# Layer 1 of a two-layer transformer block: the minus-maxima of the second half move ahead of the keys and the gate product on TensorE

## What is computed

```python
x = x + L0_xattn(_layernorm(x), ctx, ctx, ...)
x = x + L0_ffn(_layernorm(x), ...)
x = x + L1_xattn(_layernorm(x), ctx, mask, ...)
x = x + L1_ffn(_layernorm(x), ...)

def L1_xattn(x, context, mask, ...):
    q, kv = ln(x) @ Wq, ln(context) @ Wkv
    k, v = split(kv)                       # with a null key and value ahead
    sim = einsum('bhid,bhjd->bhij', q * 0.25, k)
    attn = softmax(where(mask, sim, -big))
    return ln((attn @ v) @ Wo)

def L1_ffn(x, w_gate, w_up, w_down):
    gate = silu(bitlinear(x, w_gate))
    return bitlinear(gate * bitlinear(x, w_up), w_down)
```

## Time and profile before

| | us |
|---|---|
| median of 3 runs | 889.36 |
| lowest and highest of the 3 | 884.31, 891.05 |
| the profiled execution: its time | 892.16 |
| the profiled execution: its span, first to last instruction | 890.4 |
| PE busy in the span | 831.4 (93%) |
| DVE busy | 679.9 (76%) |
| ACT busy | 433.5 (49%) |
| POOL busy | 480.8 (54%) |

### The profile page before, as it was taken

The page is one execution under the profiler, slowest core; times in us unless marked ns, Lnnn a source line. Parts: engine busy times, 40 slices in busy tenths (PEclk is TensorE's granted clock), DMA queues, the critical chain, the costliest instruction groups (busy, mean ns, idle before and its releaser), DMA issues.

```text
span 890.4 us, 28136 instructions
## 1 busy us (share of the span) xinstructions
PE 831.4 (93%) x10019; PEld 683.1 (77%) x10019; DVE 679.9 (76%) x1920; ACT 433.5 (49%) x1011; POOL 480.8 (54%) x972
## 2 busy tenths in 40 slices
PE   4999999998599997999999999999999999999964
PEld 2777777777598885788888888888888888888842
DVE  3788888876534564678888888888888888888865
ACT  1566666545055663334445454554545545445432
POOL 7567678877422224336465564655646556464331
PEclk9999999988799997999999999999999999999985
DMA  8566330001556651112112121121211212112120
GB/s 252 213 253 260 134 103 14 15 20 41 161 152 164 162 156 30 35 33 58 37 49 53 35 65 38 47 55 36 64 38 50 53 35 65 37 46 49 29 59 9
DMA packets 57980, 71.33 MB, mean 80 GB/s; under 512 B 8051, under 2 KB 34547, under 8 KB 57843
## 3 DMA queue, kind: packets, MB, share of 16 engines
q1 hardware_dynamic: 42546, 45.08, 19.4%
q10 hardware_dynamic: 13248, 20.26, 6.2%
q0 software_dynamic: 2048, 4.20, 1.6%
HBM read 45.13 MB, written 24.38 MB: 78 GB/s over the span
## 4 chain that ended last, share of the span: by engine, by line
PE 87%; DVE 5%; issue 3%; DMA 2%; ACT 1%; POOL 1%; SPq 0%; ACTq 0%; DVEq 0%; POOLq 0%
PE psum L1708 7%; PE psum L1634 7%; PE psum L1733 7%; PE psum L1684 7%; PE psum L1625 7%; PE psum L1664 6%; PE psum L975 4%; PE psum L380 4%; PE psum L965 4%; PE psum L1744 4%; PE psum L1720 4%; PE psum L387 3%; PE psum L399 3%; PE psum L371 2%; PE psum L1698 2%
## 5 line engine op out<-in xcount | busy, mean ns | idle before, releaser
L1894 ACT ACTIVATE a_pT<-psum 128x512 f32<-128x512 f32 x128 | 69.5, 594 | 67.3 <-PE psum L1720 39.7
L667 DVE TENSOR_REDUCE l_mx<-psum 128x4 bf16<-128x512 f32 x128 | 81.5, 678 | 1.9 <-PE psum L371 1.8
L2037 DVE TENSOR_REDUCE a_mxf<-psum 128x4 f32<-128x512 f32 x128 | 81.2, 675 | 2.1 <-PE psum L1698 2.0
L1634 PEld LDWEIGHTS psum<-a_cTm,a_Wk 128*128 128x128 f32 x512 | 65.0, 197 | 22.8 <-issue 21.3
L1466 POOL TENSOR_TENSOR f_hd<-f_hmc,f_wmean 128x1 f32<-128x1 f32 x32 | 6.8, 212 | 137.1 <-DVE f_hr L2150 137.1
L1625 PEld LDWEIGHTS psum<-a_xT,a_Wq 128*128 128x128 f32 x512 | 66.1, 196 | 15.3 <-issue 14.4
L502 ACT ACTIVATE l_pT<-psum 128x512 f32<-128x512 f32 x128 | 70.5, 598 | 12.4 <-PE psum L387 12.1
L1708 PE MATMUL psum<-a_qT,a_kT 64*128 64x128 f32 x1024 | 73.5, 284 | 0.0
L1634 PE MATMUL psum<-a_cTm,a_Wk 128*128 128x128 f32 x512 | 70.7, 282 | 1.9 <-POOL a_cTm L1423 1.1
L1625 PE MATMUL psum<-a_xT,a_Wq 128*128 128x128 f32 x512 | 71.1, 283 | 0.5 <-ACT a_xT L1877 0.5
L1684 PE MATMUL psum<-a_Wv,a_cTm 128*128 128x512 f32 x128 | 70.1, 630 | 1.5 <-DVE a_kT L2025 0.7
(11 more groups left out here) (300 smaller groups left out, 2228.0 us busy)
## 6 DMA issues: line engine op xcount, KB each, us to landing
sorted_x<-r_zeros ACTq DMA_DIRECT2D x12, 1408.0 KB, 5.8
a_r_all<-a_r_rows SPq DMA_DIRECT2D x64, 256.0 KB, 4.0
e_w<-in_E_W1b SPq DMA_DIRECT2D x39, 258.0 KB, 2.8
e_xt<-sorted_x SPq DMA_DIRECT2D x39, 64.0 KB, 2.4
sorted_y<-e_yt ACTq DMA_DIRECT2D x39, 64.0 KB, 2.6
a_cin<-in_ctx SPq DMA_DIRECT2D x32, 64.0 KB
out<-f_x SPq DMA_DIRECT2D x32, 64.0 KB, 3.3
x_res<-in_x SPq DMA_DIRECT2D x1, 512.0 KB, 7.3
```

The source lines that it names most:

```text
L667: nc.vector.tensor_reduce(mx[:, s, Q4 * k:Q4 * k + Q4], maxp[k % 2].rearrange("p (h t) -> p h t", h=Q4), AX_X, ALU.max).then_inc(mx_ready, 1)
L1634: last = nc.tensor.matmul(bank[:, i * S:(i + 1) * S], Wk[:, 4 * half + i, :], cTm[:, b % 2, :], start=True, stop=True)
L1894: nc.scalar.activation(pT[:, 2 * half + e, :], tp[e], ACT.Exp, scale=SCALE).then_inc(exp_ready, 1)
L2037: nc.vector.tensor_reduce(mxf[:, hh:hh + 4], maxp[e].rearrange("p (h t) -> p h t", h=Q4), AX_X, ALU.max).then_inc(mxf_ready, 1)
```

## The change

On TensorE, `minus_max(b, 1)` is called right behind `values(b, 0)`, ahead of `keys(b + 1, 0)` and `gate_part(f)`. Nothing is added or removed, and the lists of the other engines and the waits inside the functions are as they were.

```diff
                 queries(b + 1, 0)
             if b >= 1:
                 values(b, 0)
+            minus_max(b, 1)
             if more:
                 keys(b + 1, 0)
             if f is not None:
                 gate_part(f)
-            minus_max(b, 1)
             scores(b, 1)
             if more:
                 max_scores(b + 1, 0)
```

## The result

The changed kernel takes 897.77 us (median of 12 runs, 892.49 to 901.57), the kernel before 889.38 (12 runs, 884.31 to 893.07): a ratio of 1.0095, with a 95% interval of 1.0075 to 1.0116. It is slower by about 8.4 us, where 1.6 less was forecast. The profiled execution has a span of 896.1 us, 5.7 more than before; the remainder is that the profiled run of before lay 2.8 above its median.

The account below looks back on a forecast made before the run. PE was taken as the bound, 15.95 us a pass. Net -0.03 a pass (-0.08 + 0.05) over 27 passes, -0.8, with -0.45, -0.45 and +0.1 at the ends gave -1.6: 887.8 us, range 884.0 to 892.0.

Parts of the forecast that it names:

- the terms of the stretch on TensorE: Values to maximum scores on PE: 0.86 + 0.46 + 0.95 + 0.30 + 1.00 = 3.57 us, against 3.65 before.
- the ends of the loop: Passes 0 and 31: minus-maxima fit into a 0.77 us gap on PE, -0.45 us each; passes 1 to 3 together +0.1.
- the inputs of the minus-maxima are there: On PE, the moved matmuls find their inputs ready with 0.9 us left, so the move adds no wait.
- rival B: DVE's chain becomes the bound and the kernel gets slower: new wait 0.21 a pass, +2.7 us, 892.1 us; chance 0.18.
- What is pushed back: Keys and gate product start 0.37 us later, 0.45 against what follows; DVE's chain up to the second key copy moves along.
- this leaves ... 0.05: New wait of PE at the input transpose: 0.02 to 0.11 us a pass, taken as 0.05.
- The cover ahead of the input transpose: Between DVE's second key copy and PE's weight load: 0.29 us less a 0.05 step between engines, 0.24.
- The cover behind it: Hidden transposes wait for POOL 0.25 us behind the input transpose, which covers 0.10 to 0.19 of its 0.21 delay.
- The chain on DVE: From gate multiply to second key copy, no idle time on DVE; the whole chain moves by 0.45 us against PE.
- The way over POOL: POOL's scales come 0.45 us later and push rounding and hidden transposes; counted against: the rounding waited 0.40 for ACT.
- the ring over the key copy: Gate product, tanh, gate multiply, DVE steps, second key copy, input transpose, back to PE; new wait 0.05 us, or 0.21.
- TensorE's own sum: A pass on PE with all of the 0.08 us saving kept: 15.87 us, against 15.95 before.

Follow-up runs that it names:

- e6: The changed kernel with POOL's gather and residual addition ahead of the two inverse roots; 892.6 us, ratio 1.0027 to the kernel before.
- e1: The changed kernel with DVE's second key copy ahead of the denominators' inverse; 897.5 us, ratio 1.0087 to the kernel before.
- e3: The changed kernel with DVE's second key copy ahead of the inverse and POOL's rounding ahead of its scales; 889.8 us, ratio 0.9997 to the kernel before.
- e7: The kernel before with four of the eight minus-maxima ahead of the keys and POOL's gather and residual addition ahead of the inverse roots; 887.4 us, ratio 0.9961.
- e5: The kernel before with only the first four of the eight minus-maxima moved ahead of the keys; 893.9 us, ratio 1.0045.
- e2: The changed kernel with POOL's rounding of the hidden values ahead of its scales; 903.7 us, ratio 1.0178 to the kernel before.
- e8: The kernel before with POOL's gather and residual addition ahead of the two inverse roots, nothing else; 889.9 us, ratio 0.9990.

## Why the prediction was wrong

Right were the terms of the stretch on TensorE (3.57 forecast, 3.55 measured), the ends of the loop (-0.45 each; pass 0 gave 0.40, pass 31 0.44), that the inputs of the minus-maxima are there, and the mechanism of rival B, which had 0.18 and whose sign, a pass above 15.95, is what came; its price of +2.7 us was a third of the measured 8.4. What failed is the step *What is pushed back*, and in it the sum "this leaves ... 0.05".

- The cover ahead of the input transpose was sized at 0.24, with 0.05 for the step from another engine to PE. That 0.05 came from a row of POOL. From DVE's key copy to PE's load it is 0.12 (527.40 + 0.63 = 528.03, load at 528.15), so the cover was 0.29 - 0.12 = 0.17 to 0.18.
- The cover behind it, set at 0.10 to 0.19, was 0.13: the two weight loads, 0.25 apart before, stand 528.27 - 528.15 = 0.12 apart now.
- The chain on DVE was taken to move without changing its length. It grew by 0.14 in most passes, by 0.31 in three and by 0.43 in one, since the later gate multiply puts the norm beside POOL's residual addition. This term was missing altogether, in the bounds too, and e6 measures it: 16.18 - 16.04, which is 0.13 a pass before rounding.
- The way over POOL was set aside because the rounding had waited 0.40 for ACT. That slack is less than the delay of 0.45, and far less than the 0.59 that it is with the norm. e1, where only this way is left, has a pass of 16.12: POOL alone would have cost 0.17.

With these the ring over the key copy gives 0.37 (gate product later; 0.36 measured) + 0.14 - 0.18 - 0.13 = +0.20 a pass, against +0.23 measured; the rest is that the next maximum scores start 0.37 behind the hidden transposes' weight load, in place of 0.33. Rival B should have been the forecast: even without the norm's stretch the ring is 0.09 longer than the old pass, as passes 28 and 29 and e6 show. The rest of the loss in passes 4 to 30 (437.3 - 430.7 = 6.6, of which 27 x 0.23 = 6.2) is what a few passes of 16.3 to 16.5 us add and the shorter passes 28 to 30 take off.

A fault of method stands behind it: once the transposes wait for DVE, what TensorE saves elsewhere in the pass no longer counts. I set -0.08 against a new wait computed with bounds as narrow as 0.02 to 0.11, from covers read to 0.05, so the range was too narrow on the slow side. e3 and e7, with 15.86 and 15.85 a pass, show that TensorE's own sum (15.87) was right where no ring binds. That 1% was the least that could be told from no change was wrong as well: with 12 runs of each kernel the interval is 0.4% wide.

## What to carry to other kernels

On a loop spread over engines, write out each ring that leads from the moved instruction through the other engines back to the first, with its slack, before counting what the moved instruction saves; with 0.3 us of slack, a producer pushed back by 0.37 cost more than the 0.09 saved. Cover a wait of 0.07 with 0.2 us of work, not with 0.45: half of the matmuls did it (e7). And when an engine's chain shifts in time, look at what runs beside it at the new place.

## What the hardware showed that was not expected

DVE's `tensor_scalar` between SBUF tiles takes longer beside some POOL instructions. The norm step of 0.34 us took 0.44 in the kernel before, where the gather ran beside it. Timelines of DVE and POOL of the kernel before, in the pass of the earlier trace rows:

```profile
614.17 0.43 DVE L2017 TENSOR_SCALAR a_xn<-x_res,a_mv,a_rs 128x128 f32<-128x128 f32 x1
```

```profile
613.49 1.10 POOL L1372 DMA_INDIRECT xy<-sorted_y,pos_g  x1 [0.17 <-issue]
```

It ends 0.01 behind the gather's end. In the changed kernel the second step took 0.48 beside the residual addition, in e5 0.62, each 0.09 behind that addition's end, and 0.65 was the longest, beside gather and addition. POOL is slowed in its turn: in most passes of the changed kernel, where the first norm step was already under way, the addition took 0.55 in place of 0.47. The Trainium skill, "SBUF — State Buffer", section "Who interferes with whom", says that a `tensor_scalar` can run in a mode that needs a pair of ports which DVE shares with GpSimd, and that the one which issues second is then fully blocked until the other is done. No row shows in which mode DVE ran. The rows for gather and addition agree in that each stretched step ends only behind the POOL instruction beside it; but it ends 0.01 to 0.09 behind, less than the 0.34 that it takes alone, so they don't show that all of it waited. The rounding in e2 doesn't agree: the DVE step took 0.52 and was done 1.26 us before POOL's instruction of 2.03 us ended, so there it was slowed and not held to the end. The price in this loop was 0.13 us a pass where the step lies in the ring (e6), and nothing where it doesn't (e8).
